# Embedding: patch tiles loaded once, transposed and in pairs; mean from weight columns, mean square from ScalarE and TensorE

## What is computed

```python
p = p.transpose(0, 2, 4, 3, 5, 1).reshape(bsz, NP, PD)   # 64 x 36 x 768
out = layernorm(p, ln1_g, ln1_b)
out = jnp.einsum('bnp,pe->bne', out, W) + b
out = layernorm(out, ln2_g, ln2_b)
out = jnp.concatenate([cls, out], axis=1)
out = out + pos_embed                                    # 64 x 37 x 192
```

## Time and profile before

| | |
|---|---|
| median of 3 runs | 1000.62 us (994.01 to 1002.33) |
| the profiled execution: span | 1013.5 us, 12.9 us over the median; no other time of this execution is given |
| mean granted TensorE clock | 0.902 of full speed |
| TensorE busy (matmuls) | 878.3 us, 87% |
| VectorE, ScalarE, GpSimd busy | 460.6, 315.7, 279.8 us |
| embedding, from the first instruction to the end of the last y | 0 to 69.98 us |
| loads of the embedding | 22 of x (336.0 KB), 22 of xT (333.0 KB), `ca` 1062.0 KB, identity 64.0 KB |

### The profile page before, as it was taken

One profiled execution on the slowest core, in us unless ns is written; L12 is line 12 of the kernel. 1 busy time (PEld: TensorE's weight loads), 2 busy tenths in 40 slices (PEclk: granted clock), 3 DMA queues, 4 the chain that ended last, 5 costly groups with the idle time before them and its releaser, 6 DMA issues. The chain is left out here.

```text
span 1013.5 us, 18267 instructions
## 1 busy us (share of the span) xinstructions
PE 878.3 (87%) x6209; PEld 626.3 (62%) x6209; DVE 460.6 (45%) x1542; ACT 315.7 (31%) x904; POOL 279.8 (28%) x242
## 2 busy tenths in 40 slices
PE   6789999889999989886898899977465999999980
PEld 6677888666556545454654677756462666666650
DVE  5764555538533322226653588845681222222220
ACT  2444333227533222221231566633101122211210
POOL 1440000000000000000232355530018188888454
PEclk9999999779899999998995799985556999999995
DMA  8999000000079999963500000001105255555222
GB/s 246 256 296 420 5 2 2 1 1 1 2 301 421 420 420 421 421 242 101 195 8 1 1 2 1 0 1 27 48 15 144 65 102 103 101 105 92 37 24 23
DMA packets 64454, 128.52 MB, mean 127 GB/s; under 512 B 26910, under 2 KB 47184, under 8 KB 54912
## 3 DMA queue, kind: packets, MB, share of 16 engines
q1 hardware_dynamic: 34432, 118.22, 32.4%
q0 software_dynamic: 29952, 9.36, 6.9%
HBM read 115.37 MB, written 11.98 MB: 126 GB/s over the span
## 5 line engine op out<-in xcount | busy, mean ns | idle before, releaser
L1805 POOL DMA_INDIRECT out_dram<-yr,put x48 | 105.7, 2202 | 65.6 <-issue 43.7
L1259 POOL MEMSET xg<- 96x74 f32 x1 | 0.2, 157 | 420.1 <-PE bank L1233 420.1
L1869 PE MATMUL bank<-zTa,w 128*128 128x372 f32 x256 | 90.2, 497 | 0.8 <-DVE zTb L1943 0.8
L1791 POOL DMA_INDIRECT zr<-z_rows,take x48 | 66.5, 1386 | 85.9 <-issue 85.9
L1952 DVE TENSOR_TENSOR hT<-sg,bank 128x372 f32<-128x372 f32 x64 | 31.8, 539 | 107.6 <-ACT sg L1913 63.1
L1093 DVE COPY eh<-bank 128x384 f32<-128x384 f32 x32 | 17.8, 557 | 119.1 <-PE bank L1129 119.1
L1869 PEld LDWEIGHTS bank<-zTa,w 128*128 128x128 f32 x256 | 47.5, 194 | 38.2 <-ACT sg L1913 8.4
L1151 PE MATMUL bank<-w2s,eg 128*64 128x192 f32 x768 | 69.4, 330 | 0.0
L1883 PE MATMUL bank<-w2r,hT 128*124 128x192 f32 x384 | 66.1, 330 | 0.8 <-DVE hT L1952 0.8
L1883 PEld LDWEIGHTS bank<-w2r,hT 128*124 128x124 f32 x384 | 61.9, 187 | 3.8 <-issue 3.8
L1913 ACT ACTIVATE sg<-bank 128x372 f32<-128x372 f32 x64 | 27.3, 478 | 115.6 <-PE bank L1874 115.6
(11 more groups left out here) (287 smaller groups left out, 1766.0 us busy)
## 6 DMA issues: line engine op xcount, KB each, us to landing
w1s<-in_w_dram SPq DMA_DIRECT2D x32, 1152.0 KB, 12.7
w2s<-in_w_dram SPq DMA_DIRECT2D x32, 1152.0 KB, 14.8
w<-in_w_dram SPq DMA_DIRECT2D x8, 1024.0 KB, 7.8
xt<-in_x_dram SPq DMA_DIRECT2D x22, 336.0 KB, 9.1
xT<-in_xT_dram SPq DMA_DIRECT2D x22, 333.0 KB, 8.3
ys<-eo SPq DMA_DIRECT2D x64, 48.0 KB, 10.0
w2r<-in_w2r_dram SPq DMA_DIRECT2D x8, 384.0 KB, 4.7
e<-ys SPq DMA_DIRECT2D x21, 96.0 KB, 2.0
```

The costliest lines, as they stand in the source:

```text
L1791: nc.gpsimd.indirect_dma_start(zr[b][:, j, :], None, z_rows, bass.IndirectOffsetOnAxis(ap=take[:, k:k + 1], axis=0), bounds_check=NROW - 1 ...
L1805: nc.gpsimd.indirect_dma_start(rows_out, bass.IndirectOffsetOnAxis(ap=put[:, k:k + 1], axis=0), yr[e % 2][:, j, :], None, bounds_check=OUT ...
L1869: nc.tensor.matmul(bank[to + 2 * part + half][:, 0:HS], w13[b][:, 0, at:at + 128], zTa[b][:, half * HS:(half + 1) * HS], start=True, stop= ...
```

## The change

The row-wise copy of x is no longer loaded. The transposed tiles come two per transfer (128 x 2 x 6 x 111), 11 transfers into a ring of four pairs; a pair's place is free when both the products and the squares of its tiles are done. The weights get two more columns of 1/768, so that the product gives each row's mean in column 192. ScalarE squares the transposed tile (128 x 666, `xsq`); VectorE adds the six chunks (`xss`, 128 x 111); TensorE multiplies that by a column of 1/768 and puts the mean square into column 256 of the tile's bank. VectorE makes the variance from the two in three operations on one column. Four PSUM banks are used in turn instead of two. The constants come in two transfers: gains, biases and weights first, the rows of biases and positions later; TensorE makes the column sums first and the bias product second. The first load of tiles stands between the two transfers of constants.

Core of the diff (declarations and the host's layout of x left out):

```diff
         def embed_sp(sp):
-            sp.dma_start(ca[:], ins["ca"]).then_inc(s_ca, 16)
-            sp.dma_start(ident, ins["ident"]).then_inc(s_ca, 16)
-
-            def load_x(t, q):
-                if after(t, 4):
-                    sp.wait_ge(s_xst, t - 3)
-                sp.dma_start(xt[q][:], ins["x"][t]).then_inc(s_x[q], 16)
-                if after(t, 4):
-                    sp.wait_ge(s_typ, t - 3)
-                sp.dma_start(xT[q][:], ins["xT"][t]).then_inc(s_xr[q], 16)
-
-            over_tiles(sp, [(0, load_x)], T, unroll=4)
+            first = colA["btok"][1]
+            sp.dma_start(ca[:, 0:first], ins["ca"][:, 0:first]).then_inc(s_ca, 16)
+
+            def load_x(p, q):
+                if p >= 4:
+                    sp.wait_ge(s_typ, 2 * p - 6)
+                    sp.wait_ge(s_xsq, 2 * p - 6)
+                sp.dma_start(xT[q][:], ins["xT"][p]).then_inc(s_xr[q], 16)
+
+            load_x(0, 0)
+            sp.dma_start(ca[:, first:nA], ins["ca"][:, first:nA]).then_inc(s_ca2, 16)
+            sp.dma_start(ident, ins["ident"]).then_inc(s_ca2, 16)
+            for p in range(1, T // 2):
+                load_x(p, p % 4)
             sp.dma_start(cb[:], ins["cb"]).then_inc(s_cbi, 16)
             sp.dma_start(cc[:], ins["cc"]).then_inc(s_cci, 16)
 
...
+            nc.gpsimd.memset(mean_of[:], 1.0 / PD)
+            nc.gpsimd.memset(wtok_c[:, :, ED:ED + 2], 1.0 / PD)
...
+            def square_x(t, q):
+                b = q % 2
+                act.wait_ge(s_xr[q // 2], (t - q) * 2 + 16)
+                if after(t, 2):
+                    act.wait_ge(s_xss, t - 1)
+                nc.scalar.activation(xsq[b][:], xT[q // 2][:, q % 2], ACT.Square).then_inc(s_xsq, 1)
+
+            def std_x(t, q):
+                b = q % 2
+                act.wait_ge(s_xvar, t + 1)
                 if after(t, 2):
                     act.wait_ge(s_xrs, t - 1)
-                nc.scalar.activation(xsd[b][:], xmv[b][:, 1:2], ACT.Sqrt, bias=eps5[0:TP, :]).then_inc(s_xsd, 1)
-
-            def std_y(t, b):
+                nc.scalar.activation(xsd[b][:], xvar[b][:], ACT.Sqrt, bias=eps5[0:TP, :]).then_inc(s_xsd, 1)
+
+            def std_y(t, q):
+                b = q % 2
                 act.wait_ge(s_y, t + 1)
                 nc.scalar.activation(ysq[b][:], y[b][:], ACT.Square, accum_out=yss[b][:]).then_inc(s_yss, 1)
...
-            over_tiles(act, [(0, std_x), (1, std_y), (2, norm_y)], T)
+            over_tiles(act, [(0, square_x), (2, std_x), (3, norm_y), (2, std_y)], T, unroll=8)
...
+            def sum_x(t, q):
+                b = q % 2
+                dve.wait_ge(s_xsq, t + 1)
+                if after(t, 2):
+                    dve.wait_ge(s_xps, t - 1)
+                nc.vector.tensor_reduce(xss[b][:], xsq[b][:].rearrange("p k t -> p t k"), AX.X, ALU.add).then_inc(s_xss, 1)
+
+            def mean_x(t, q):
+                b = q % 2
+                dve.wait_ge(s_xps, t + 1)
+                nc.vector.tensor_scalar(xm1[b][:], bank[2 + q % 4][0:TP, ED:ED + 1], -1.0, None, ALU.mult).then_inc(s_xm1, 1)
+
+            def mean_square_x(t, q):
+                b = q % 2
+                dve.wait_ge(s_xm1, t + 1)
+                nc.vector.tensor_scalar(xm2[b][:], bank[2 + q % 4][0:TP, ED:ED + 1], xm1[b][:], None, ALU.mult).then_inc(s_xm2, 1)
+
+            def var_x(t, q):
+                b = q % 2
+                dve.wait_ge(s_xm2, t + 1)
                 if after(t, 2):
                     dve.wait_ge(s_xsd, t - 1)
-                nc.vector.bn_stats(xst[b][:, 0, :], xt[q][0:TP, 0:PD // 2])
-                nc.vector.bn_stats(xst[b][:, 1, :], xt[q][0:TP, PD // 2:PD]).then_inc(s_xst, 1)
-
-            def mean_var_x(t, q):
-                b = q % 2
-                dve.wait_ge(s_xst, t + 1)
-                nc.vector.memset(tick[:, 4:5], 0.0)
-                nc.vector.bn_aggr(xmv[b][:], xst[b][:]).then_inc(s_xmv, 1)
+                nc.vector.tensor_scalar(xvar[b][:], bank[2 + q % 4][0:TP, 256:257], xm2[b][:], 0.0, ALU.add, ALU.max).then_inc(s_xvar, 1)
 
...
+            centred_weights()
             for t in range(2):
-                stats_x(t, t)
-                mean_var_x(t, t)
-                if t == 0:
-                    centred_weights()
-            centred_bias()
-
-            def first_x(t, q):
-                if after(t, 2):
-                    stats_x(t, q)
-
-            def first_mean_x(t, q):
-                if after(t, 2):
-                    mean_var_x(t, q)
-
-            over_tiles(dve, [(1, rstd_x), (0, first_x), (1, bias_y), (0, first_mean_x), (2, rstd_y), (4, stats_h)], T, unroll=4)
+                sum_x(t, t)
+            token_rows()
+
+            def later_sum_x(t, q):
+                if after(t, 2):
+                    sum_x(t, q)
+
+            over_tiles(dve, [(2, mean_x), (0, later_sum_x), (2, mean_square_x), (3, rstd_y), (2, var_x), (5, stats_h), (2, rstd_x), (2, bias_y)], T, unroll=8)
 
...
             def product(t, q):
-                pe.wait_ge(s_xr[q], (t - q) * 4 + 16)
-                if after(t, 2):
-                    pe.wait_ge(s_y, t - 1)
+                pe.wait_ge(s_xr[q // 2], (t - q) * 2 + 16)
+                if after(t, 4):
+                    pe.wait_ge(s_y, t - 3)
                 for k in range(KC):
-                    last = nc.tensor.matmul(bank[2 + q % 2][0:TP, 0:ED], xT[q][:, k, :], wtok_c[:, k, :], start=(k == 0), stop=(k == KC - 1))
+                    last = nc.tensor.matmul(bank[2 + q % 4][0:TP, 0:ED + 2], xT[q // 2][:, q % 2, k, :], wtok_c[:, k, :], start=(k == 0), stop=(k == KC - 1))
                 last.then_inc(s_typ, 1)
 
-            over_tiles(pe, [(0, product)], T, unroll=4)
+            def square_means(t, q):
+                pe.wait_ge(s_xss, t + 1)
+                nc.tensor.matmul(bank[2 + q % 4][0:TP, 256:258], xss[q % 2][:], mean_of[:], start=True, stop=True).then_inc(s_xps, 1)
+
+            over_tiles(pe, [(0, product), (1, square_means)], T, unroll=8)
 
```

More of the change, by code:

```diff
@@ L186, in tower @@
         wtok = A["wtok"].rearrange("p (k e) -> p k e", k=KC)
-        xt = [sb(f"xt{q}", [TR, PD]) for q in range(4)]
-        xT = [sb(f"xT{q}", [128, KC, TP]) for q in range(4)]
+        xT = [sb(f"xT{q}", [128, 2, KC, TP]) for q in range(4)]
+        xsq = [sb(f"xsq{b}", [128, KC, TP]) for b in range(2)]
+        xss = [sb(f"xss{b}", [128, TP]) for b in range(2)]
+        mean_of = sb("mean_of", [128, 2])
         row_sum = sb("row_sum", [128, KC])
@@ L197, in tower @@
         pos_bias = sb("pos_bias", [TP, ED])
-        xst = [sb(f"xst{b}", [TP, 2, 6]) for b in range(2)]
-        xmv = [sb(f"xmv{b}", [TP, 2]) for b in range(2)]
+        xm1 = [sb(f"xm1{b}", [TP, 1]) for b in range(2)]
+        xm2 = [sb(f"xm2{b}", [TP, 1]) for b in range(2)]
+        xvar = [sb(f"xvar{b}", [TP, 1]) for b in range(2)]
         xsd = [sb(f"xsd{b}", [TP, 1]) for b in range(2)]
@@ L463, in tower @@
         s_brg = sem("attn_gated")
-        s_ca = sem("constants_a_in")
+        s_ca = sem("token_weights_in")
+        s_ca2 = sem("token_rows_in")
         s_eps = sem("eps_set")
@@ L470, in tower @@
         s_pb = sem("pos_bias_ready")
-        s_x = [sem(f"x_in{q}") for q in range(4)]
-        s_xr = [sem(f"xT_in{q}") for q in range(4)]
+        s_xr = [sem(f"xT_pair_in{q}") for q in range(4)]
         s_rs = sem("wtok_row_means")
         s_wc = sem("wtok_centred")
-        s_xst = sem("x_stats")
-        s_xmv = sem("x_mean_var")
+        s_xsq = sem("x_squared")
+        s_xss = sem("x_squares_summed_by_row")
+        s_xps = sem("x_square_means")
+        s_xm1 = sem("x_mean_negated")
+        s_xm2 = sem("x_mean_squared")
+        s_xvar = sem("x_var")
         s_xsd = sem("x_std")
@@ L622, in centred_weights, with token_rows @@
                 dve.wait_ge(s_cb, 1)
+                total = bank[6][:, 0:ED].unsqueeze(1).to_broadcast([128, KC, ED])
+                nc.vector.scalar_tensor_tensor(out=wtok_c[:, :, 0:ED], in0=total, scalar=-1.0 / PD, in1=wtok_g[:], op0=ALU.mult, op1=ALU.add).then_inc(s_wc, 1)
+            def token_rows():
+                dve.wait_ge(s_ca2, 32)
+                dve.wait_ge(s_cb, 2)
                 nc.vector.tensor_tensor(tok_sum[:], A["btok"], bank[7][0:TP, 0:ED], ALU.add).then_inc(s_tb, 1)
+                nc.vector.tensor_tensor(pos_bias[:], A["pos"], A["b2m"], ALU.add).then_inc(s_pb, 1)
                 dve.wait_ge(s_tb, 1)
                 nc.vector.bn_stats(tok_st[:], tok_sum[:]).then_inc(s_tb, 1)
-                dve.wait_ge(s_cb, 2)
-                total = bank[6][:, 0:ED].unsqueeze(1).to_broadcast([128, KC, ED])
-                nc.vector.scalar_tensor_tensor(out=wtok_c[:], in0=total, scalar=-1.0 / PD, in1=wtok_g[:], op0=ALU.mult, op1=ALU.add).then_inc(s_wc, 1)
+                dve.wait_ge(s_pb, 1)
+                nc.vector.tensor_tensor(pos_bias[:], pos_bias[:], A["cls"], ALU.add).then_inc(s_pb, 1)
                 dve.wait_ge(s_tb, 2)
```

(26 more changed lines are left out.)

13 lines of the change are left out of this document (3 added, 10 removed).

## The result

The changed kernel takes **1044.54 us** in the median (1043.47 to 1051.63, 4 runs) against 1001.48 us before on the same chip (994.01 to 1011.46, 4 runs): a ratio of 1.0438, 95% interval 1.0392 to 1.0485. Forecast were 1032 us, between 1017 and 1046. The profiled run took 1044.24 us, span 1042.3 us. The kernel before varies from run to run, over three comparisons from 992.08 us (mean granted clock 0.924) to 1011.46 us, and ratios are taken over the fast runs alone while medians are over all runs, so that a ratio need not be the quotient of two medians.

What follows compares the result with a forecast made beforehand. Transfers were taken to bound the embedding at 2.7 us a tile. Start 20.6, nineteen turns of 4.07 and two of 1.75 put the last y at 101.4 us, +31.4 on the 1000.62 median: 1032 us, range 1017 to 1046.

Steps and rivals of the forecast that it cites:

- Transfers end as the bound: Embedding: without row-wise x, transfers take 1.25 us a tile, under every other term, so waiting for them ends.
- The circle: Embedding: ScalarE and VectorE wait for each other within each turn, so turns cannot overlap; 4.07 us a tile against 2.7.
- the stride: VectorE's reduction: extra price for adding elements 111 apart, taken as 0.3 us on top of 0.84, giving 1.14.
- The VectorE row that I named: Profile row of a 22-element VectorE operation, inputs six apart against side by side: 0.6 ns an element more.
- The upper bound of 1.51 us: VectorE's strided reduction at most, from ScalarE's transposing store costing 1.0 ns an element more than a plain one.
- The start: Embedding's beginning: constants at 4.6 us, centred weights at 12.1, first mean read at 18.0, first y at 20.6.
- The end: Embedding's last y at 101.4 us instead of 69.98, shifting all later work by 31.4 us.
- closing turn: Embedding's two last turns, without square and reduction: 1.75 us each.
- The identity products: 36 TensorE products behind the last y, ahead of the attention's transposes; no lengthening in the sum, up to 4 us possible.
- rival 2: Embedding: TensorE loses its clock and becomes the bound, 4.6 us a tile, shift +46, 1047 us; chance 0.11.
- Rivals 1 and 3: Embedding: dearer strided reduction, 1039 us, chance 0.19; or busiest engine, TensorE at 2.35 us a tile, sets pace, 997 us, 0.08.
- rival 1: VectorE's strided reduction costs the full extra nanosecond an element, 1.51 us, period 4.44, 1039 us; chance 0.19.

Runs made afterwards that it cites:

- pairs: Kernel before with both copies of x loaded two tiles per transfer, statistics still row-wise on VectorE; 1004.15 us against 1004.58, ratio 1.0002.
- pairs and early start: Kernel before with both x copies two tiles per transfer, token weights loaded first, centred weights ahead of the first statistics; 1003.92 us against 1005.67, ratio 0.9983.
- three additions: Changed kernel with three additions, last in VectorE's turn, replacing the reduction, and ScalarE's normalization one turn later; 1022.57 us against 1005.67 for the kernel before, ratio 1.0209.
- clock kept: Changed kernel with filling identity products on TensorE, 12 per tile from tile 15 and 48 behind the last tile; 1045.76 us in one run.

## Why the prediction was right

**Transfers end as the bound: held.** No wait for x is left in the trace, and 1.25 us a tile were never near the period.

**The circle: held, and this decided.** By the starts in the turn shown (the last two rows from the turn's own y, 52.85, to the square at 53.99):

| link | forecast, us | measured, us |
|---|---|---|
| square, to reduction | 0.83 | 0.78 |
| reduction and small operations, to root | 1.49 | 1.69 |
| root, to reciprocal | 0.37 | 0.32 |
| reciprocal, to y | 0.20 | 0.26 |
| y, to its square | 0.43 | 0.45 |
| square and root of y, to next square | 0.75 | 0.69 |
| sum | 4.07 | 4.19 |

The link that was most off is that of the reduction, by 0.20 us; the others together are 0.08 shorter than forecast. I took 0.3 us for the stride, and it is 0.43; contiguous I had 0.84, and it is 0.846. The VectorE row that I named, 0.6 ns an element, gives 0.40 us for 666 elements and would have been nearly right; for going below it I gave no reason. The other 0.07 us lie in the small operations and the hand-over to ScalarE. The upper bound of 1.51 us, from ScalarE's transposing store, was not reached. The Trainium skill, "Advanced Engine Details and Errata", section SBUF Cachelines, says without a figure that reads which take a new line each time lose speed; here they do, by 0.65 ns an element. That the circle is what binds, and not the work in it, the reduction put last shows: 4.19 falls to 2.81 with the durations kept.

**The start: 0.9 us better than forecast.** The constants were there at 4.82 (4.6), the centred weights at 12.17 (12.1), but the bias products ended 0.8 us earlier than I had them and the first mean was read at 16.88 (18.0). The first y is done at 19.73 (20.6 in the sum).

**The end.** From 19.73, nineteen full turns of 4.19 and closing ones of 2.18 and 2.19 give 103.7; I had 1.75 for a closing turn. Against the sum that is -0.9 at the start, 19 times 0.12 or +2.3 in the turns, and +0.9 at the close: the last y shifts by 33.75 us where 31.4 were forecast. That the errors at the start and at the close cancel is chance.

**The identity products: the term left at nothing.** The 2.6 us more stood in rival 2 as a possibility ("up to 4 us longer") and belong in the sum. The last turns hold no products, and the clock is at 0.50 when the identity products begin. The rest of rival 2 fell as argued: the clock swings between 0.50 and 1.00 in the stage, and y stays 4.19 apart. Two products of the changed kernel, one tile after the other:

```profile
57.60 4.10 PE L807 MATMUL bank<-wtok_c,xT 128*111 128x194 f32 x12 [0.97 <-DVE y L696]
...
61.78 2.20 PE L807 MATMUL bank<-wtok_c,xT 128*111 128x194 f32 x12
```

The first runs at the lower level and takes nearly twice as long; the second starts 4.18 us behind it all the same. With the clock at 1.00 and 1.5 us more work per tile it stays so too.

**Rivals 1 and 3.** The reduction of 1.51 us and the circle of 4.44 were not reached. A period under 2.5 us was not reached by any order tried; with the circle undone VectorE holds it at 2.81. Even then the change is slower than the kernel before (1.5 to 2.9%), whose transfers give 2.7.

**The total: inside the range, in part by luck.** The prediction gave 1019 to 1036 us for a circle of 3.5 to 4.25 us. The circle came out inside, at 4.19, and the time outside, at 1044.54; the stated range holds it because it reaches on to 1046 for a dearer reduction or part of rival 2. By the total alone rival 1 (1039) and rival 2 (1047) were nearer than 1032, and only the trace decides against them. Of the 12.5 us between 1032 and 1044.54, 2.35 are the later last y, 2.6 the identity products, 0.9 the median of the kernel before (1001.48 in place of 1000.62), and 6.7 are the rest.

**The rest.** The attention begins 36.35 us later, the median is 43.1 us longer in that comparison; 1001.48 + 36.35 would be 1037.8. The remaining 6.7 us I can't assign. A part may be the scatter of four runs each: over 13 and 16 runs the kernel before had medians of 1004.58 and 1005.67, from which 36.35 more would be 1040.9 and 1042.0. The profiled runs show no place where more is lost. Starts of the same products in four of them, in us:

| products (line in the kernel before) | before | the change | pairs | pairs and early start |
|---|---|---|---|---|
| attention's first transposes (798) | 78.17 | 114.52 | 72.17 | 71.33 |
| experts' first (1125) | 275.11 | 311.48 | 266.38 | 264.11 |
| neighbourhood attention, keys (1508) | 515.50 | 552.08 | 507.00 | 504.48 |
| neighbourhood attention, values (1527) | 550.05 | 580.23 | 535.13 | 539.04 |
| end of the span | 1013.5 | 1042.3 | 997.2 | 1002.5 |

The change is some 36.5 us behind up to the keys and then 30.2: between the two products the kernel before is at a clock of 0.50 from 534 us on and the change still at 1.00. This low-clock stretch lasts 37.5 us in the kernel before and, from 580 us on, 23.9 in the change. The profiled run of the kernel before, with a span of 1013.5 us, is longer than any measured run of it, so the difference of the two spans, 28.9 us, is no measure of the change. From the first transposes on, where the kernels are alike, the profiled runs need 935.3 us (before), 927.8 (the change), 925.0 (pairs), 931.2 (pairs and early start), 923.6 (three additions), 922.1 (clock kept): the later stages alone vary by 13 us.

Two versions whose embedding is shorter by 6 and 7 us do not measure as faster, though in their profiled runs the lead is not given back: at the keys it has grown to 8.5 and 11.0. Whether their later stages run at a lower clock on the average, or the medians only scatter by that much, stays open: the mean granted clock over the runs of the last comparison is 0.908 for the pairs with early start and 0.910 for the kernel before, too close to tell. No version beats the kernel before beyond its interval.

## What to carry to other kernels

When a bound is taken away, follow the two queues that share a tile through one whole turn: where each waits in the middle of its turn for the other's step of the same turn, the period is the sum of both, however idle each looks. Put the step that waits for the longest foreign operation last in its queue, and then check that the engine's own work still fits the old period. Less traffic pays only down to the next limit: here 2.7 us of transfers a tile gave way to 2.81 us of VectorE's work in the best order tried, and to 4.19 in the order of the change.

## What the runs showed of the hardware

- A VectorE reduction of 128x666 fp32 in groups of six takes 846 ns with the six side by side and 1280 ns with them 444 bytes apart: 0.65 ns an element.
- Two VectorE additions that write in place take 0.56 us for 333 columns and 0.54 us for 111; one of 111 columns into another buffer takes 0.28 us. Why the middle one is so long wasn't tried; writing in place is not enough for it, since an in-place addition of 192 columns (`pos_bias`, kernel before) takes 0.36 us and one into another buffer 0.35.
- Transfers of two tiles instead of one, with the same bytes in all and rings that hold twice the tiles, raise the rate of the stage from 258 to 302 GB/s; which of the two does it was not tried.
- In the embedding of the change TensorE at a granted clock of 0.50 (1.2 GHz) cost time only where its work was on the path: 2.6 us at the identity products, nothing in turns whose product takes 4.10 us instead of 2.20.
